# Tile 0 of a sparse graph-attention kernel: from the dense path to four list tiles made of column strips

## The chip, the cores and the metric

The kernel runs on one core of a Trainium2 chip. Its time is what one execution takes on the device, in microseconds (us). Three executions of the kernel before took 2577.2, 2580.97 and 2586.93 us; the median is 2580.97 us. One more execution was profiled, and its rows are the ones read here. Engines are called PE (TensorE), DVE (VectorE), ACT (ScalarE), POOL (GpSimd) and SP (the queue that only issues DMAs).

## The reference

`x` is 8192x256, `adj` 8192x8192 and mostly zero. With `h = relu(layernorm(x))` the layer is graph attention with 8 heads of 32:

```python
h = (x @ W.T).reshape(n, H, D)
s_src = einsum('nhd,hd->nh', h, a_src); s_dst = einsum('nhd,hd->nh', h, a_dst)
attn = s_src[:, None, :] + s_dst[None, :, :] + adj[:, :, None] * We[:, 0] + be
attn = where(adj[:, :, None] > 0, attn, -inf)
attn = softmax(leaky_relu(attn, 0.2), axis=1)
return x + einsum('ijh,jhd->ihd', attn, h).reshape(n, 256) + x @ Wr.T + br      # x in "x @" is relu(layernorm(x))
```

The probability of an edge between rows i and j falls with both numbers (as 1/sqrt of each). So row 0 has 738 neighbours, and the largest counts of tiles 0 to 11 (128 rows each) are 738, 75, 61, 58, 50, 43, 41, 39, 35, 36, 35 and 29. Within a row the neighbours are dense on the left and sparse on the right.

## The kernel before

**Prologue.** 32 steps of 256 rows each. DVE normalizes (`normalize`, lines 561 to 580), PE transposes and multiplies (`turn`, `maps`, lines 1047 to 1073), ACT copies out of PSUM, DVE adds the biases (`add_biases`, line 582), POOL stores the rows of `table` (features and destination scores), of `dst_rows` (the same scores transposed, for the dense path), of `resid` and of `out`. DVE and PE of neighbouring steps overlap.

**List tiles.** Tiles 1 to 63 are sparse enough for lists. For each, SP loads its 4 MB of `adj` in 8 pieces into one of two buffers. DVE *finds* (line 614): it cuts the 8192 columns into 7 to 35 segments, takes the 8 largest of each (line 632) with their columns (line 624) and packs them into keys (lines 636 to 651). It *sorts* (line 653): K//8+1 rounds over the keys give up to K neighbours a row. If a segment or the list might have held more, the tile's flag is set.

**Dealing.** From tile 4 on, tiles stand in groups (line 46). DVE counts the rows' neighbours (`count`, 690) and ranks them (`place`, 713, with matmuls at 1103), POOL scatters the lists by rank to HBM (`deal`, 514) and loads them back (`load_dealt`, 524). So the rows with the most neighbours share a tile, and the later tiles of the group have shorter lists: the K values in `GROUPS`. Tiles 1, 2 and 3 (`DIRECT`) are not dealt; they take 75, 61 and 58 slots.

**Units.** A list tile, dealt or direct, is a unit u. POOL gathers K table rows for each of the 128 rows of the unit, one indirect DMA a slot (`gather`, 488; line 500), into a ring of 86 slots. A slot is free when the matmuls that summed its last content are done; at most four gathers are in flight. ACT prepares the scores, DVE does the softmax in steps (`softmax_step`, 732) and multiplies most slots by their weights (`weight`, 762, line 769), ACT the rest (961), PE sums the slots (1085), DVE evacuates (772), POOL adds the result into `out` (`store`, 505, line 509), three units late.

**The order.** All orders are written out. DVE's loop (lines 784 to 812) does, for unit u, finds until `found[u]` tiles are found (table `FOUND`, line 57, then u+13), the last of them interleaved with unit u's softmax. `plan` (line 112) fixes after which unit's gather a group is dealt and loaded. POOL's loop is at 535.

**Dense path.** Tile 0 keeps its flag at 1 from the start (line 435). At the end the flags are read (820, 320), and each flagged tile is computed against all 8192 columns, head by head (`dense_tile`, 408, 828, 974, 1142). For these inputs that is tile 0 alone.

Of the kernel before, what the change touches and what calls it, by code (L numbers as in the profile page):

```python
# [22 lines left out]
P = 128  # L23
N = 8192
# [21 lines left out]
GROUPS = ((4, (50, 32, 28, 24)),  # L46
# [12 lines left out]
GMAX = max(len(ks) for _, ks in GROUPS)  # L59
KLIST = max(ks[0] for _, ks in GROUPS)  # L60
KMAX = 8 * (max(DIRECT) // 8 + 1)
VMAX = 8 * max(n for n, _ in SEGS.values())
WIDE = max(len(ks) * (HEAD + 2 * ks[0]) for _, ks in GROUPS)
RANKS = max(len(ks) * (ks[0] + 1) for _, ks in GROUPS)
# [6 lines left out]
class Source:  # L71


    def __init__(self, t, K, group, place):
        self.t, self.K, self.group, self.place = t, K, group, place
        self.segs, self.power = SEGS[max(a for a in SEGS if a <= t)]
        self.rounds = K // 8 + 1


class Unit:  # L80


    def __init__(self, u, K, source, group, place):
        self.u, self.K, self.source, self.group, self.place = u, K, source, group, place
        self.act_slots = K // 2 if K < 18 else 10 if K < 20 or K > 38 else 14 if K < 32 else 16
        self.parts = 2 if K < 30 else 3 if K < 40 else 8
# [15 lines left out]
class Group:  # L102


    def __init__(self, g, t0, ks):
        self.g, self.t0, self.ks, self.n, self.K = g, t0, ks, len(ks), ks[0]
        self.W, self.D = HEAD + 2 * ks[0], ks[0] + 1
        self.first = t0 - FIRST
        self.listed = t0 + self.n - FIRST


def plan():
    sources = [Source(FIRST + i, K, None, None) for i, K in enumerate(DIRECT)]
    units = [Unit(i, K, sources[i], None, None) for i, K in enumerate(DIRECT)]
    groups = []
    for g, (t0, ks) in enumerate(GROUPS):
        group = Group(g, t0, ks)
        groups.append(group)
        for i, K in enumerate(ks):
            sources.append(Source(t0 + i, group.K, group, i))  # L120
            units.append(Unit(len(units), K, None, group, i))

    found = [FOUND[u] if u < len(FOUND) else min(len(sources), u + LEAD) for u in range(len(units))]
    for group in groups:
        group.ranked_at = min(u for u in range(len(units)) if found[u] >= group.listed)
        group.placed_at = min(group.ranked_at + 1, group.first - 2)
        group.at_once = group.placed_at == group.ranked_at
# [3 lines left out]
    at, owner, part_sums, acts, issued = 0, [None] * GSLOTS, 0, 0, 0  # L131
    for un in units:
# [14 lines left out]
        if un.u >= LATE:  # L147
            units[un.u - LATE].store_seq = issued
            issued += 1
        for group in groups:  # L150
# [9 lines left out]
    return sources, units, groups, found  # L160
# [10 lines left out]
def gat_kernel(nc, x, adj, W, We, be, a_src, a_dst, Wr, br, out):  # L171
    table = nc.dram_tensor("table", (N + PAD, ROW), F32, kind="Internal").ap()
    resid = nc.dram_tensor("resid", (N, HD), F32, kind="Internal").ap()
    dst_rows = nc.dram_tensor("dst_rows", (H, N), F32, kind="Internal").ap()

    with ExitStack() as ctx:
        sources, units, groups, found = plan()
# [13 lines left out]
        ps_dst = banks[:, 2:6, 384:512].rearrange("p (u b) n -> p u b n", u=2)  # L191
# [14 lines left out]
        br_all = sb("br_all", [P, HD])  # L206
        be_all = sb("be_all", [P, H])
        we_all = sb("we_all", [P, H])
        seg_base = {(n, w): sb(f"seg_base{n}_{int(10 * w)}", [P, n * 8]) for n, w in sorted({(so.segs, so.power) for so in sources})}
# [17 lines left out]
        own = [sb(f"own{i}", [P, HEAD + 2 * K]) for i, K in enumerate(DIRECT)]  # L227
# [9 lines left out]
        limits = spare(len(GROUPS) * (KLIST + 1)).rearrange("p (g d) -> p g d", d=KLIST + 1)  # L237
        valid = spare(GMAX * KLIST)
# [23 lines left out]
        def part(width):  # L262
# [11 lines left out]
        dst_sb = part(2 * 2 * P).rearrange("p (u b n) -> p u b n", u=2, b=2)  # L274
# [22 lines left out]

        S = {n: sem(n) for n in (
            "ones_set", "held", "ident_set", "blk_zero", "blk_in", "w_in", "small_in", "wt_done", "wt_copied",
            "x_in0", "x_in1", "x_in2", "x_in3", "x_free", "bn_done", "mv_done", "sd_done", "eps_set", "rstd_done", "hn_done", "hnT_ps", "hnT_done",  # L300
            "proj_done", "hd_copied", "dst_copied", "s_done", "res_done", "br_added",
# [915 lines left out]
```

## Time and profile before

| | |
|---|---|
| median of 3 executions | 2580.97 us (2577.2 to 2586.93) |
| span of the profiled execution | 2582.7 us (the only figure there is for it; it stands 1.7 us above the median) |
| busy | DVE 2124.4 us (82%), POOL 1488.1 (58%), ACT 1246.3 (48%), PE 1240.2 (48%) |
| largest groups | gathers x1137 (line 500), segment maxima x624 (632) and their columns x624 (624) |
| DMA | 512.8 MB in 226533 packets, 199 GB/s mean |

The profile gives each engine's busy time and, for each instruction, the idle time before it with what ended it. POOL's busy time leaves out about 0.3 us between two gathers, which the rows call "issue": an engine 77% busy with gathers can be full. Stages are best read apart, since the engines' shares differ from one to the next.

### The profile page before, as it was taken

The numbers are of one execution on the slowest core, as the hardware profiler recorded it, in microseconds if no ns is written. First come the engines' busy times: TensorE is split into PE (matmuls) and PEld (weight loads), VectorE is DVE, ScalarE is ACT, GpSimd is POOL, SyncE is SP. The second block draws the span as 40 slices with busy tenths as digits, with TensorE's granted clock in tenths as the row PEclk, the third lists the DMA queues.
The fourth block names the chain that finished last, engine by engine and source line by source line (L and its number), as shares of the span: only waits on it lengthen the run. The fifth ranks groups of instructions, "written<-read, shape, count | busy, mean of one in ns | idle before, by whom it ended". The sixth has DMA issues, their size and how long they took to land.

```text
span 2582.7 us, 27816 instructions
## 1 busy us (share of the span) xinstructions
PE 1240.2 (48%) x5305; PEld 938.2 (36%) x5306; DVE 2124.4 (82%) x4852; ACT 1246.3 (48%) x4898; POOL 1488.1 (58%) x1666
## 2 busy tenths in 40 slices
PE   6991013504325267426634543443443364528885
PEld 4661013403314145314522432332332252416664
DVE  3558969999898998979998999999999921279991
ACT  1320030203335598639656555645634666826662
POOL 4772756656774677777777777656646657700000
PEclk9996557657656576656666665666666666759997
DMA  3667767686776877777787878778878424486660
GB/s 110 193 206 242 224 139 213 175 234 187 194 238 187 260 221 224 211 224 221 239 259 229 256 239 269 242 230 253 251 213 258 137 51 101 90 232 164 166 159 3
DMA packets 226533, 512.83 MB, mean 199 GB/s; under 512 B 98280, under 2 KB 116400, under 8 KB 224208
## 3 DMA queue, kind: packets, MB, share of 16 engines
q1 hardware_dynamic: 151280, 319.60, 39.2%
q0 software_dynamic: 74960, 191.61, 29.1%
q14 instruction: 116, 0.95, 0.1%
q8 instruction: 33, 0.54, 0.1%
q10 hardware_dynamic: 144, 0.13, 0.0%
HBM read 475.19 MB, written 36.03 MB: 198 GB/s over the span
## 4 chain that ended last, share of the span: by engine, by line
DMA 24%; issue 23%; DVE 12%; POOL 10%; PE 5%; ACT 4%; POOLq 0%; DVEq 0%; ACTq 0%; PEldq 0%; SPq 0%
DMA arena<-table,arena 18%; POOL arena L500 8%; DVE work L632 4%; ACT arena L961 3%; DMA out_dram<-w_all,arena 3%; DVE work L624 2%; PE banks L1115 1%; DMA lists<-arena,rank 1%; PE banks L1168 1%; DVE arena L769 1%; PE banks L1158 1%; DMA adj_sb<-in_adj_dram 1%; POOL lists L519 1%; DMA arena<-lists 1%; PE banks L1093 1%
## 5 line engine op out<-in xcount | busy, mean ns | idle before, releaser
L500 POOL DMA_INDIRECT arena<-table,arena x943 | 974.3, 1033 | 397.8 <-issue 237.3
L1093 PE MATMUL banks<-arena,ident 128*128 128x256 f32 x1268 | 420.2, 505 | 1030.7 <-DVE arena L769 1030.7
L961 ACT ACTIVATE arena<-arena,prob 128x32 f32<-128x32 f32 x4024 | 859.5, 306 | 2.0
L1093 PEld LDWEIGHTS banks<-arena,ident 128*128 128x128 f32 x1268 | 326.0, 263 | 1121.4 <-issue 884.4
L624 DVE FIND_INDEX8 work<-work,adj_sb 128x8 uint32<-128x184 f32 (+51 forms) x624 | 629.9, 1012 | 0.0
L632 DVE MAX8 work<-adj_sb 128x8 f32<-128x184 f32 (+51 forms) x624 | 620.4, 1002 | 0.7 <-DMA adj_sb<-in_adj_dram 0.4
L956 ACT ACTIVATE prob<-pre 128x104 f32<-128x104 f32 (+26 forms) x63 | 20.2, 321 | 866.4 <-DVE pre L753 866.4
L1099 PE MATMUL banks<-arena,ident 128*128 128x256 f32 x1006 | 317.4, 447 | 109.7 <-ACT arena L961 109.2
L500 POOL DMA_INDIRECT arena<-table,own x194 | 204.1, 1052 | 142.0 <-issue 47.4
L1099 PEld LDWEIGHTS banks<-arena,ident 128*128 128x128 f32 x1006 | 200.8, 216 | 215.0 <-ACT arena L961 192.5
L946 ACT ACTIVATE pre<-arena,we_all 128x13 f32<-128x13 f32 (+23 forms) x480 | 146.5, 400 | 78.6 <-DMA arena<-lists 78.6
L769 DVE TENSOR_TENSOR arena<-arena,prob 128x768 f32<-128x768 f32 (+7 forms) x158 | 183.1, 1208 | 0.0
L742 DVE TENSOR_TENSOR pre<-pre,arena 128x80 f32<-128x80 f32 (+20 forms) x76 | 19.8, 274 | 182.3 <-DMA arena<-table,arena 112.0
L509 POOL DMA_INDIRECT out_dram<-w_all,arena x60 | 98.5, 1642 | 44.2 <-DVE w_all L779 16.9
L519 POOL DMA_INDIRECT lists<-arena,rank x60 | 59.7, 996 | 110.2 <-DVE rank L726 86.6
L1115 PE MATMUL banks<-work,ones 128*128 128x24 f32 (+6 forms) x404 | 92.6, 384 | 0.0
L1115 PEld LDWEIGHTS banks<-work,ones 128*128 128x128 f32 x404 | 89.2, 323 | 0.0
L1168 PE MATMUL banks<-ident,adj_sb 128*128 128x128 f32 x256 | 44.7, 305 | 62.7 <-ACT adj_sb L989 62.7
L1072 PE MATMUL banks<-w_all,arena 128*128 128x256 f32 x256 | 73.0, 408 | 0.0
L1158 PE MATMUL banks<-pre,work 128*32 128x128 f32 x512 | 72.7, 289 | 0.0
L1066 PE MATMUL banks<-w_all,arena 128*128 128x272 f32 x256 | 70.1, 397 | 0.0
L850 DVE TENSOR_TENSOR arena<-arena 128x4096 f32<-128x4096 f32 x16 | 70.0, 4417 | 0.0
(140 smaller groups left out, 1795.8 us busy)
## 6 DMA issues: line engine op xcount, KB each, us to landing
adj_sb<-in_adj_dram SPq DMA_DIRECT2D x504, 512.0 KB, 4.5
arena<-dst_rows SPq DMA_DIRECT2D x16, 2048.0 KB, 8.7
arena<-table,arena POOLq DMA_INDIRECT x943, 4.1
table<-arena POOLq DMA_DIRECT2D x32, 264.0 KB, 2.9
arena<-in_x_dram SPq DMA_DIRECT2D x32, 256.0 KB, 3.0
resid<-arena POOLq DMA_DIRECT2D x32, 256.0 KB, 2.6
out_dram<-arena POOLq DMA_DIRECT2D x32, 256.0 KB, 2.8
work<-table SPq DMA_DIRECT2D x8, 1024.0 KB, 11.8
```

The costliest lines, as they stand in the source:

```text
L500: pool.indirect_dma_start(gath[:, un.slot(k), :], None, table[:, :], bass.IndirectOffsetOnAxis(ap=rec[:, k, 0:1], axis=0), bounds_check=N ...
L509: pool.indirect_dma_start(out[:, :], bass.IndirectOffsetOnAxis(ap=record(un)[:, 0:1].bitcast(U32), axis=0), out_sb[:, un.u % OUTS, :], Non ...
L519: pool.indirect_dma_start(lists[group.g][:, :], bass.IndirectOffsetOnAxis(ap=rank[:, group.g % 2, i:i + 1], axis=0), stage[:, group.g % 2, ...
L624: v.max_index(idx8[:, 8 * s:8 * s + 8], val8[:, 8 * s:8 * s + 8], a[:, bounds[s]:bounds[s + 1]]).then_inc(S["scanned"], 1)
L632: v.max(val8[:, 8 * s:8 * s + 8], a[:, bounds[s]:bounds[s + 1]]).then_inc(S["maxed"], 1)
L769: last = v.tensor_tensor(gv, gv, pb.unsqueeze(3).to_broadcast([P, n, H, D]), ALU.mult)
L946: last = s.activation(pv[:, h, :], pairs(rec, K)[:, :, 1], ACT.Identity, scale=we_all[:, h:h + 1], bias=rec[:, 1 + h:2 + h])
L961: last = s.activation(g, g, ACT.Copy, scale=prob[:, b, k * H + h:k * H + h + 1])
L1093: last = m.matmul(ps_sum[:, u % 2, :], ident[:, :], gath[:, un.slot(k), 0:HD], start=(k == 0), stop=False)
L1099: last = m.matmul(ps_sum[:, u % 2, :], ident[:, :], gath[:, un.slot(k), 0:HD], start=False, stop=(k == K - 1))
L1115: m.matmul(rv[:, i, :], ones[:, :], same[:, j * D:(j + 1) * D], start=False, stop=(i == n - 1 and j == i - 1))
L1158: last = m.matmul(ps_acc[:, b, :], hv[:, 4 * q + r, :], pt_sb[q % 4][:, r * P:(r + 1) * P], start=(q == 0 and r == 0), stop=(q == 15 and r ...
```

## The change

Tile 0 no longer goes through the dense path. Its 128 rows are cut into pieces of a row: rows 0 to 7 into 16 column strips, rows 8 to 23 into 8, rows 24 to 47 into 4, rows 48 to 127 into 2 (strip edges at N·w²/n², so that each holds about as many neighbours). The 512 pieces (cut into 37, 29, 46 and 39 segments over 992, 1920, 6144 and 6144 columns for the finds) are four list tiles ("windows") of 128 pieces each. Their sources stand first, as group 0 with K = 60, 37, 29, 22; tiles 1 to 3 become a dealt group with K = 75, 48, 39. The finds and sorts of the windows stand between the prologue's steps on DVE: steps 2 to 29 each get a seventh of one window. The window units store an unnormalized-by-tile result and the maxima and sums per head to HBM; after the last find, SP loads them by row, DVE and ACT combine the parts, and POOL adds the 128 rows to `out`. `dst_rows` is no longer written in the prologue (its matmuls, line 1069, its copy, 918, and its DMA, 467, are gone); the dense path, if a tile is flagged, would fetch it from `table`. The prologue's loops on SP and DVE are unrolled. Both `adj` buffers are set to zero on POOL at the start, and POOL fills 151 more 8-column segment bases there; before its first work DVE adds each piece's first column to them, in 17 one-column operations and 4 wide ones that wait for POOL's `ids`. Counted on the reference's matrix, no piece has more than 60 neighbours, no segment of a window that is checked has more than 7, and the rows above each K are at most as many as the tiles before it hold (124 of 128, 242 of 256, 371 of 384 for the windows; 122 of 128 and 246 of 256 for tiles 1 to 3).

```diff
+WINDOWS = (((0, 8, 16),), ((8, 24, 8),), ((24, 48, 4), (48, 64, 2)), ((64, 128, 2),))
+WINDOW_AT = ((0, 6144), (1, 6144), (0, 0), (1, 0))
+WINDOW_K = (60, 37, 29, 22)
...
+WINDOW_EXACT = (4, 1, 1, 0)
...
-GROUPS = ((4, (50, 32, 28, 24)),
+GROUPS = ((1, (75, 48, 39)),
+          (4, (50, 32, 28, 24)),
-DIRECT = (75, 61, 58)
-FOUND = (4, 7, 10, 12, 15, 16, 18, 20, 21, 22)
+FOUND = (7, 9, 10, 11, 14, 16, 18, 20, 21, 22)
...
-        group.placed_at = min(group.ranked_at + 1, group.first - 2)
+        group.placed_at = group.ranked_at + 1
```

On SP:

```diff
+            for u in range(4):
+                load_x(u)
+            sp.wait_ge(S["window_zero"], 2)
+            for k in range(NV):
+                so = sources[k]
+                for p, r0, r1, c0, c1 in so.windows():
+                    sp.dma_start(adj_sb[p:p + r1 - r0, so.buf, so.col:so.col + c1 - c0], adj[r0:r1, c0:c1]
+                                 ).then_inc(S[f"window_in{k}"], 16)
+            for u in range(4, 8):
+                load_x(u)
+            sp.wait_ge(S["s_done"], 1)
+            sp.dma_start(own_scores[:, :], s_all[:, 0, :]).then_inc(S["own_out"], 16)
+            sp.wait_ge(S["own_out"], 16)
+            for k in range(NV):
+                for p, r0, r1, c0, c1 in sources[k].windows():
+                    sp.dma_start(window_scores[p:p + r1 - r0, k, :], own_scores[r0:r1, :]).then_inc(S["own_in"], 16)
+            for u in range(8, UNITS):
+                load_x(u)
```

On POOL:

```diff
-            pool.memset(flags[:, :], 1.0).then_inc(S["flag_init"], 1)
+            for so in sources[:NV]:
+                for n in range(so.segs):
+                    last = pool.memset(window_base[so.c][:, 8 * n:8 * n + 8], float((so.bounds[n] + PAD) << JBITS))
+            for b in range(2):
+                pool.memset(adj_sb[:, b, :], 0.0).then_inc(S["window_zero"], 1)
-                    pool.wait_ge(S["dst_copied"], u + 1)
-                    pool.dma_start(dst_rows[:, bass.ts(u, 2 * P)].rearrange("h (b p) -> h b p", b=2),
-                                   dst_sb[0:H, q, :, :]).then_inc(S[f"dst_out{q}"], 16)
+            deal(groups[0])
+            load_dealt(groups[0])
             for un in units:
                 gather(un)
                 if un.u >= LATE:
                     store(units[un.u - LATE])
+                if un.u == comb_store_at:
+                    pool.wait_ge(S["comb_done"], 1)
+                    pool.dma_start(out[0:P, :], comb_out, accum_op=ALU.add).then_inc(S["comb_out"], 16)
```

On DVE:

```diff
+            dve.wait_ge(S["ids_set"], 1)
...
+            def windows_beside(u):
+                c, m = (u - 2) // 7, (u - 2) % 7
+                if u < 2 or c >= NV:
+                    return
+                segs, steps = sources[c].segs, 2 * sources[c].rounds
+                if m < 4:
+                    scan(c, segs * m // 4, segs * (m + 1) // 4)
+                if m == 4:
+                    keys(c)
+                if m >= 4:
+                    for step in range(steps * (m - 4) // 3, steps * (m - 3) // 3):
+                        sort_step(c, step)
+                if m == 6:
+                    decode(c)
+
+            for u in range(UNITS):
+                normalize(u, u % 4)
+                windows_beside(u)
+                if u >= 2:
+                    add_biases(u - 2, (u - 2) % 4)
+            add_biases(UNITS - 2, 2)
+            count(groups[0])
+            add_biases(UNITS - 1, 3)
+            place(groups[0])
...
+                if un.u == comb_clear_at:
+                    combine_clear()
+                if un.u == comb_shift_at:
+                    combine_shift()
+                if un.u == comb_out_at:
+                    combine_out()
```

On PE:

```diff
-                    for c in range(2):
-                        rows = hnT[:, q, b, c * P:(c + 1) * P]
-                        m.matmul(ps_dst[0:H, q, b, :], w_all[:, c, HD:ROW], rows, start=(c == 0), stop=(c == 1))
```

## Rows read from the trace of the kernel before

**Rows 1.** Busy time of each engine, PE clock and DMA by stage.

```profile
core 0: us, PE busy (x) PEld busy (x) DVE busy (x) ACT busy (x) POOL busy (x), PEclk, DMA share, GB/s
...
20.30:206.90 186.60, 178.79 (x896) 123.25 (x896) 90.39 (x288) 54.24 (x129) 125.16 (x156) 1.00 0.60 193
206.90:822.00 615.10, 173.58 (x712) 148.24 (x712) 566.20 (x1621) 143.32 (x627) 368.32 (x352) 0.62 0.71 199
822.00:1154.00 332.00, 151.98 (x482) 109.33 (x482) 294.80 (x707) 215.49 (x975) 237.80 (x226) 0.63 0.76 232
1154.00:2010.00 856.00, 388.63 (x1262) 292.46 (x1262) 833.96 (x1844) 500.58 (x2239) 576.52 (x542) 0.64 0.80 242
2010.00:2266.00 256.00, 128.49 (x394) 94.74 (x393) 98.54 (x267) 170.15 (x754) 170.13 (x156) 0.66 0.37 88
2266.00:2582.60 316.60, 215.19 (x1544) 166.80 (x1544) 238.87 (x121) 162.51 (x176) 0.00 (x0) 0.84 0.58 147
```

**Rows 2.** Timeline around 2262 us: the last store, then the dense tile's first load.

```profile
2262.05 1.57 POOL L509 DMA_INDIRECT out_dram<-w_all,arena  x1 [3.55 <-DVE w_all L779]
...
2266.15 0.34 SPq L411 DMA_DIRECT2D adj_sb<-in_adj_dram  x1
```

**Rows 3.** Timeline of DVE, one step of the prologue to the next.

```profile
47.84 0.75 DVE L566 BATCH_NORM_STATS2 arena<-arena 128x6 f32<-128x256 f32 x2 [0.38 <-DVE arena L591]
...
52.04 0.17 DVE L585 TENSOR_TENSOR s_all<-arena,be_all 128x16 f32 x1 [1.75 <-ACT arena L917]
...
53.24 0.43 DVE L566 BATCH_NORM_STATS2 arena<-arena 128x6 f32<-128x256 f32 x1 [0.36 <-DVE arena L591]
```

**Rows 4.** Timeline of PE in one such step.

```profile
61.79 0.60 PE L1052 MATMUL banks<-ident,arena 128*128 128x128 f32 x4
...
63.24 0.60 PE L1069 MATMUL banks<-arena,w_all 128*8 128x128 f32 x4
63.77 1.13 PE L1072 MATMUL banks<-w_all,arena 128*128 128x256 f32 x4
```

**Rows 5.** Timeline of DVE: find and sort of tile 1, end of tile 2's find.

```profile
207.00 0.24 DVE L632 MAX8 work<-adj_sb 128x8 f32<-128x8 f32 x2 [0.45 <-DMA adj_sb<-in_adj_dram]
...
230.71 0.19 DVE L636 TENSOR_REDUCE flag<-work 128x1 f32<-128x35 f32 x1
...
232.63 0.45 DVE L662 MAX8 work<-work 128x8 f32<-128x280 f32 x1
...
250.40 0.26 DVE L632 MAX8 work<-adj_sb 128x8 f32<-128x12 f32 x2
...
272.39 0.17 DVE L636 TENSOR_REDUCE flag<-work 128x1 f32<-128x26 f32 x1
```

**Rows 6.** Timeline of POOL at the start.

```profile
0.92 0.20 POOL L432 MEMSET ones<- 128x128 f32 x1 [0.29 <-POOLq L1204]
...
1.24 5.37 POOL L439 MEMSET seg_base<- 128x8 f32 x155
```

**Rows 7.** Gathers (line 500) by stretch: POOL busy time, their count, clock, DMA.

```profile
251.00:358.00 107.00, 75.32 (x76) 0.50 0.76 211
358.00:557.70 199.70, 128.77 (x119) 0.65 0.69 179
572.00:780.00 208.00, 140.36 (x134) 0.66 0.74 211
```

**Rows 8.** Timeline of POOL: the deal and the load before tile 8.

```profile
801.36 1.02 POOL L519 DMA_INDIRECT lists<-arena,rank  x1 [20.34 <-DVE rank L726]
...
816.04 0.95 POOL L532 DMA_DIRECT2D arena<-lists  x1 [3.93 <-DMA lists<-arena,rank]
...
821.84 1.06 POOL L500 DMA_INDIRECT arena<-table,arena  x1 [4.84 <-DMA arena<-lists]
```

**Rows 9.** The page's groups: stores of a unit, and DVE's weighting.

```profile
L769 DVE TENSOR_TENSOR arena<-arena,prob 128x768 f32<-128x768 f32 (+7 forms) x158 | 183.1, 1208 | 0.0
...
L509 POOL DMA_INDIRECT out_dram<-w_all,arena x60 | 98.5, 1642 | 44.2 <-DVE w_all L779 16.9
```

More of the change, by code:

```diff
@@ L147, in plan @@
         if un.u >= LATE:
-            units[un.u - LATE].store_seq = issued
-            issued += 1
-        for group in groups:
+            done = units[un.u - LATE]
+            done.store_seq = issued
+            issued += 2 if done.partial else 1
+        for group in groups[1:]:
             if group.dealt_after == un.u:
@@ L159, in plan @@
         issued += 1
-    return sources, units, groups, found
+    return sources, units, groups, found, issued
 def segments(n, power):
@@ L352, in listed, with own_head, loads_before @@
         def listed(eng, un):
-            if un.group is None:
-                eng.wait_ge(S["decoded"], un.u + 1)
-            else:
-                landed(eng, un.group.load_seq + 1)
+            landed(eng, un.group.load_seq + 1)
+        def own_head(group):
+            if group.t0 is None:
+                return ids[:, 0:NV], window_scores[:, :, :], window_flags[:, :]
+            rows = slice(group.t0, group.t0 + group.n)
+            return ids[:, rows], s_all[:, rows, :], flags[:, rows]
         segs_before = [sum(so.segs for so in sources[:c]) for c in range(len(sources))]
         def scans_of(so, n):
-            return sum(lo < (n + 1) * PIECE for lo in segments(so.segs, so.power)[:-1])
+            return sum(lo < (n + 1) * PIECE for lo in so.bounds[:-1])
+        def loads_before(so):
+            return sum(o.t is not None and o.buf == so.buf for o in sources[:so.c])
+        last_find = min(u for u in range(len(units)) if found[u] == len(sources))
+        comb_clear_at, comb_shift_at, comb_out_at, comb_store_at = (last_find + i for i in (0, 2, 3, 5))
         load_adj = lambda t: adj[bass.ts(t, P), :]
@@ L674, in decode @@
                 t, K, rec = so.t, so.K, staged(so)
-                if so.group is not None and so.place == 0 and so.group.g >= 2:
+                if so.place == 0 and so.group.g >= 2:
                     before = groups[so.group.g - 2]
@@ L686, in decode @@
                 dve.wait_ge(S["flag_a"], c + 1)
-                v.tensor_tensor(flags[:, t:t + 1], flag8[:, :], slot_lo[:, K:K + 1].bitcast(F32), ALU.max
+                flag = own_head(so.group)[2][:, so.place:so.place + 1]
+                v.tensor_tensor(flag, flag8[:, :], slot_lo[:, K:K + 1].bitcast(F32), ALU.max
                                 ).then_inc(S["flag_b"], 1)
@@ L784, in _ @@
             for un in units:
-                at_once = [group for group in groups if group.at_once and group.ranked_at == un.u]
-                while done_finds < found[un.u] - (not at_once):
+                while done_finds < found[un.u] - 1:
                     find(done_finds)
@@ L791, in _ @@
                     done_finds += 1
-                for group in at_once:
-                    count(group)
                 c = done_finds if done_finds < found[un.u] else None
```

337 lines of the change are left out of this document (220 added, 117 removed), and 9 rows, old and new, of the table WINDOW_SEGS.

## The prediction

> **What bounds the kernel now.** I read the stages first [rows 1], then the end [rows 2], the gathers by stretch [rows 7], and single timelines for prices. The rows show four regimes. In the prologue (20.3 to 206.9 us) PE is busy 178.8 of 186.6 us and DVE only 90.4: PE sets the step of 186.6/32 = 5.83 us. From 206.9 to 822 DVE is busy 92%, with finds running ahead of the first units, whose gathers POOL starts at 251. From 822 to 1154, where the lists are dealt but still long, DVE falls to 89% while POOL has 226 operations in 332 us; each takes about 1.02 us and leaves 0.3 us between two, so 1.3 us at best and 1.47 us here: POOL is full and DVE waits for its gathers. From 1154 to 2010 DVE is busy 97%. After the last find POOL is again the slower one, to the last store at 2262 [rows 2]. Then the dense tile has the chip to itself from 2266.2 to the end of the span, 316.5 us, in which POOL does nothing [rows 1, 2].
>
> **The dense tile: -314 us.** Nothing lies beside it, so all 316.5 us go if no tile is flagged. The counts on the reference's matrix say that none is: 60 neighbours at most in a piece, 7 at most in a checked segment, and every K has room for its ranks. The engines still read the flags beside the landing of the last store; I put 2 us on that (0 to 5).
>
> **The start: +16 us.** POOL's segment bases cost 5.37 us for 155, 0.035 each started one behind the other; 151 more are 5.3 us. Zeroing both buffers is two writes 8192 wide: 128 columns took 0.20 us and 8 columns about 0.10, so 0.8 ns a column and 6.6 us each [rows 6]. The ids that DVE now waits for come behind both, 18.5 us later than the bases' old end at 6.6 plus 0.5 us of small work: at 25.6. DVE's 21 small operations, most in a chain of dependent ones, I put at 0.3 us each: 6 us. The weights' copies, at 14.5 us before, thus wait until about 31. Bounds: 5 (if the zeroing overlaps or is faster) to 20.
>
> **The prologue's steps: +79 us.** Removed is line 1069 on PE: 0.53 us twice a step [rows 4], so PE needs 5.83 - 1.06 = 4.8 us. Also gone are one ACT copy and one POOL DMA a step; neither engine bound, so they are worth nothing. Added on DVE is the work of four windows. Finds: tile 1's 35 segments took 23.7 us and tile 2's 26 took 22.0, both over 8192 columns [rows 5]; so 0.19 us a segment and 2.08 ns a column. The windows have 151 segments and 15200 columns: 28.7 + 31.6 = 60 us. Keys: 1.92 us at 280 wide [rows 5]; four of 232 to 368, 8 us. Sorts: tile 1's ten rounds took 17.8 us [rows 5], 1.78 each; 4 x 8 rounds, a little wider on average, at 1.9: 61 us. Decoding 2 us. Sum 131 us, or 4.7 in each of 28 steps. DVE's own part of a step is 53.24 - 47.84 = 5.40 us less 1.75 of waiting for ACT [rows 3], 3.65 us. So DVE becomes the bound: 28 x 8.35 = 234, the other four steps at 5.4 = 22, and count, rank and place of group 0, about 25 small operations and one round over PE, 8: 264 instead of 186.6, +77. SP issues 32 window loads and, later, 32 score loads between the loads of x; x(8) stands behind the second lot. At 0.5 us an issue that is 16 us, while x(8) is due three steps (25 us) after they can start: nearly hidden, 2 us. Prologue and start end DVE's part at 207 + 16 + 79 = 302 us, +95. Bounds +65 (131 us partly filling waits that I count twice, a cheap start) to +125.
>
> Here a rule speaks against the change. The clock in the prologue was 1.00, PE's 2.4 GHz level, with PE busy 96%; in the list stages, with PE busy 28 to 50%, its mean was 0.62 to 0.66; in the dense stage, at 68%, 0.84 [rows 1]. After the change PE is busy 4.8 of 8.35 us, and much of each step is one idle stretch. The Trainium skill, "TensorE: Matmul & The Clock Gate", section "Part 1: The HAM clock gate", says that a stretch without matmuls puts the array back to half rate until it has been busy again. By that rule the steps would partly run at the 1.2 GHz level, and with PE as the bound the sum would be some 25 us longer, inside my range. The rows alone give the price: 4.8 us at the lower level is 9.6 us, against 8.35 for DVE; a mix of the two levels, as the dense stage shows it, stays under 8.35, so I add nothing.
>
> **POOL's queue up to tile 8: +134 us on top.** Before, tile 8's first gather began at 821.84 [rows 8], 615 us after the prologue. In the new order, counted from DVE's end of the prologue: POOL's last stores of the prologue 6; four deals, landing and load, 15 (from 801.36 to 821.84 eight deals and one load took 20.5 [rows 8]): 21. 148 window gathers: the 76 from 251 us on took 1.41 us each with nothing in their way, the next 119 took 1.68 with ring waits and slow landings [rows 7]; the windows lie between, nearer the first because their predecessors are short: 1.45, 215 us. Two stores of the first window, 1.64 + 0.3 each [rows 9], three deals and a load: 14. 162 gathers of tiles 1 to 3 at 1.55 (the mean of both stretches was 1.58), 251. Stores of three windows, 12, and the deal and load of the next group, 11. So tile 4 starts at +524. Tiles 4 to 7 took 208 us [rows 7]; deal and load for tile 8 then take 17, without the 20.3 us that POOL waited for DVE's ranks [rows 8], since those are now made a unit earlier and DVE is ahead. 749 against 615: +134. Bounds: 85 (all at 1.41) to 165 (all at 1.68).
>
> DVE's own addition in this stage is small: the windows put 94 slots on it and tiles 1 to 3 take 32 off; at 1.208/3 = 0.40 us a slot [rows 9] that is 25 us, softmax steps some 5 us. So DVE idles for what POOL is later. From tile 8 on, orders, lead and K values are as before; POOL was the bound there until 1154 and DVE, in lockstep with it, after. I see no place where 134 us would be won back.
>
> **The combining: +2 us.** It has two operations 4096 wide, 6.4 us each by the 1.208 us of a 768 wide one [rows 9], and small ones, and lies after the last find, where DVE is busy 98.5 of 256 us. POOL waits for it two units later. If that cover were gone it would cost 15 us. ACT's added share (54 slots) has room: 143 of 615 us busy.
>
> **Sum,** against the profiled execution: 2582.7 - 314 + 16 + 79 + 134 + 2 = 2500 us. I round to 2495, which also takes off the 1.7 us by which the median of the three runs is lower.
>
> **Rivals.**
> - *Finds hide the gathers (15%).* If POOL's queue is no bound up to tile 8, because DVE's finds take the time anyway (92% busy there), only DVE's 30 us come on top instead of 134: 2390 us. For it: DVE's share up to 822. Against: 116 more gathers have no room in a stretch where POOL's 352 operations, at 1.3 us each, already fill 458 of the 571 us from 251 to 822 [rows 1].
> - *Slow gathers (13%).* The early gathers all run at the 1.68 us of the second stretch [rows 7], since SP's loads of adj take the same DMA engines (0.71 busy): 310 x 0.15 = 46 more, 2541 us.
> - *Lockstep in the prologue (5%), the slower side.* DVE's chunk, 8.35 us, and PE's part at the lower clock, 9.6, stand one behind the other in each step instead of side by side, in that DVE waits in `normalize` or `add_biases` for what PE could only start after the chunk. Then a step is 18 us, 28 x 9.6 = 270 us more: 2765. It makes the kernel slower as soon as a step passes about 11.5 us. Against it: `add_biases(u-2)` and `normalize(u)` ask for results of two steps back.
> - *The dense tile runs after all (2%).* A flag stays set; then 316 us return with a slow fetch of the transposed scores: over 2811 us.
> - The forecast: 60%. The other 5% are mishaps between these.
>
> **How the numbers follow.** The forecast's own bounds are 2495 - 30 - 49 = 2416 and 2495 + 30 + 31 = 2556, and with the slow gathers 2541 lies inside. The finds-hide case at 2390 is left out with the slower ones: 2415 to 2555 holds about 75 to 80%. About 0.5%, 13 us, is what a measurement of this kernel can tell from no change. Faster by more than that (below 2568): 60 + 15 + 13 + part of the rest = 91%, of which I keep 0.89; within 0.5%, 0.03; slower 0.08.
>
> **What the profile would show.** Right: no instruction of the dense lines; DVE near 90% busy in the prologue, its steps about 8.3 us, ending near 300 us; PE's clock there at or under 1.00; first gather near 323 us; tile 4's first gather near 825, tile 8's near 1050; DVE waiting for gathers up to tile 16; the last find near 2240 and the last store near 2495. Wrong: a prologue that ends after 330 or a step over 10 us; gathers at 1.6 us or more; DVE with no idle time before the softmax of tiles 1 to 7, in which case the time would be nearer 2390.

## The result, and the profile after

The change makes the kernel faster: 2503.4 us (median of 4 executions, 2501.01 to 2509.92) against 2583.66 for the kernel before beside it. The ratio is 0.9694, 95% interval [0.9674, 0.9714]. The forecast was 2495, its range 2415 to 2555. Some executions of a kernel are over 1.5% longer than its fastest; the ratios leave these out, the medians don't. The profiled execution has a span of 2500.6 us, 82.1 less than before.

Stages of the kernel after: the prologue; up to tile 4's first gather; up to tile 8's; up to the end of the stretch in which DVE waits for gathers; up to about the last finds; the tail. The columns are those of [rows 1].

```profile
core 0: us, PE busy (x) PEld busy (x) DVE busy (x) ACT busy (x) POOL busy (x), PEclk, DMA share, GB/s
35.00:295.00 260.00, 164.70 (x666) 130.81 (x666) 212.50 (x971) 43.77 (x97) 109.82 (x128) 0.87 0.51 157
295.00:824.00 529.00, 143.77 (x586) 120.43 (x586) 487.22 (x1454) 149.19 (x658) 349.55 (x332) 0.62 0.69 203
824.00:1047.00 223.00, 93.34 (x376) 75.16 (x376) 158.37 (x361) 97.40 (x439) 159.50 (x148) 0.66 0.63 181
1047.00:1380.00 333.00, 150.86 (x483) 108.99 (x483) 253.42 (x608) 218.97 (x992) 243.72 (x231) 0.63 0.69 205
1380.00:2240.00 860.00, 392.45 (x1279) 292.23 (x1280) 838.71 (x1856) 508.57 (x2275) 578.86 (x544) 0.64 0.80 243
2240.00:2491.00 251.00, 118.38 (x378) 88.29 (x376) 104.72 (x237) 158.63 (x703) 167.35 (x150) 0.66 0.36 81
```

The dense stage of [rows 1] has no counterpart. The prologue took 186.6 us and takes 260, with DVE busy 82% instead of 48%. From 824 to 1380 DVE, which was about 90% busy in those tiles before, is at 74%.

The next rows come from the timelines of DVE and POOL in the kernel after. They are DVE's first step and its first find behind the prologue, then POOL's first window gather, its first gathers of tiles 4 and 8 (line 596), and its last store.

```profile
35.09 0.74 DVE L702 BATCH_NORM_STATS2 arena<-arena 128x6 f32<-128x256 f32 x2
...
294.90 0.23 DVE L753 MAX8 work<-adj_sb 128x8 f32<-128x8 f32 x2
```

```profile
317.21 1.05 POOL L596 DMA_INDIRECT arena<-table,arena  x1 [7.42 <-DMA arena<-lists]
...
824.18 1.06 POOL L596 DMA_INDIRECT arena<-table,arena  x1 [4.14 <-issue]
...
1046.59 1.06 POOL L596 DMA_INDIRECT arena<-table,arena  x1 [4.43 <-issue]
...
2485.15 1.56 POOL L615 DMA_INDIRECT out_dram<-w_all,arena  x1 [3.15 <-DVE w_all L914]
```

They give the ledger. The left column is what the sum of the prediction had.

| term | forecast | measured, from the rows |
|---|---|---|
| DVE starts later | +16 | 35.09 - 20.3 = +14.8 |
| the prologue's steps and group 0's ranks | +79 | (294.90 - 35.09) - (207.00 - 20.3) = +73.1 |
| POOL's queue from there to tile 8 | +134 | (1046.59 - 294.90) - (821.84 - 207.00) = +136.9 |
| from tile 8 to the last store | +2 | (2485.15 - 1046.59) - (2262.05 - 821.84) = -1.7 |
| after the last store | -314 | (2500.6 - 2485.15) - (2582.7 - 2262.05) = -305.2 |
| sum | -83 (2500, given as 2495) | -82.1 |

Whether each term's reason holds is another matter, and that took the experiments.

### The profile page after: what moved, and what is told of

Its sections match the earlier page's. It is cut to its first block, busy times and chain, and to the rows that moved or that the text cites. A ratio compares the mean times of both kernels' runs of the same rounds, so it can differ in the third digit from the quotient of the medians.

```text
span 2500.6 us, 24906 instructions
## 1 busy us (share of the span) xinstructions
PE 1067.0 (43%) x3781; PEld 819.3 (33%) x3782; DVE 2061.7 (82%) x5509; ACT 1176.6 (47%) x5159; POOL 1638.2 (66%) x1929
## 3 DMA queue, kind: packets, MB, share of 16 engines
q14 instruction: 132, 1.08, 0.1%
## 4 chain that ended last, share of the span: by engine, by line
DMA 20%; issue 17%; POOL 10%; DVE 6%; ACT 2%; PE 2%; POOLq 0%; DVEq 0%; ACTq 0%
DMA arena<-table,arena 17%; POOL arena L596 9%; ACT arena L1160 2%; DVE work L753 2%; DMA out_dram<-w_all,arena 2%; DVE work L742 1%; PE banks L1314 1%; POOL lists L625 1%; PE banks L1292 1%; DMA lists<-arena,rank 1%; DVE arena L904 1%; POOL out_dram L615 0%; POOLq L596 0%; PE banks L1312 0%; PE banks L1298 0%
## 5 line engine op out<-in xcount | busy, mean ns | idle before, releaser
L596 POOL DMA_INDIRECT arena<-table,arena x1253 | 1308.7, 1044 | 533.5 <-issue 329.3
L1292 PE MATMUL banks<-arena,ident 128*128 128x256 f32 x1392 | 454.0, 500 | 1170.7 <-DVE arena L904 1170.7
L1160 ACT ACTIVATE arena<-arena,prob 128x32 f32<-128x32 f32 x4456 | 951.5, 307 | 2.2
L1292 PEld LDWEIGHTS banks<-arena,ident 128*128 128x128 f32 x1392 | 354.4, 260 | 1268.1 <-issue 1018.8
L742 DVE FIND_INDEX8 work<-work,adj_sb 128x8 uint32<-128x502 f32 (+56 forms) x775 | 669.7, 866 | 0.0
L753 DVE MAX8 work<-adj_sb 128x8 f32<-128x502 f32 (+56 forms) x775 | 658.6, 857 | 0.0
L1298 PE MATMUL banks<-arena,ident 128*128 128x256 f32 x1114 | 347.2, 444 | 121.2 <-ACT arena L1160 120.6
L1298 PEld LDWEIGHTS banks<-arena,ident 128*128 128x128 f32 x1114 | 219.1, 213 | 236.0 <-ACT arena L1160 212.7
L1145 ACT ACTIVATE pre<-arena,we_all 128x13 f32<-128x13 f32 (+27 forms) x536 | 165.1, 406 | 104.5 <-DMA arena<-lists 104.5
L904 DVE TENSOR_TENSOR arena<-arena,prob 128x768 f32<-128x768 f32 (+8 forms) x166 | 200.7, 1258 | 0.0
L1314 PE MATMUL banks<-work,ones 128*128 128x24 f32 (+8 forms) x422 | 90.0, 365 | 0.0
L795 DVE MAX8 work<-work 128x8 f32<-128x56 f32 (+11 forms) x290 | 81.4, 281 | 5.3
L796 DVE MAX8 work<-work 128x8 f32<-128x56 f32 (+11 forms) x290 | 77.0, 266 | 0.0
## 6 DMA issues: line engine op xcount, KB each, us to landing
adj_sb<-in_adj_dram SPq DMA_DIRECT2D x1, 1536.0 KB, 23.1
```

The costliest lines, as they stand in the source:

```text
L596: pool.indirect_dma_start(gath[:, un.slot(k), :], None, table[:, :], bass.IndirectOffsetOnAxis(ap=rec[:, k, 0:1], axis=0), bounds_check=N ...
L742: v.max_index(idx8[:, 8 * s:8 * s + 8], val8[:, 8 * s:8 * s + 8], a[:, bounds[s]:bounds[s + 1]]).then_inc(S["scanned"], 1)
L753: v.max(val8[:, 8 * s:8 * s + 8], a[:, bounds[s]:bounds[s + 1]]).then_inc(S["maxed"], 1)
L904: last = v.tensor_tensor(gv, gv, pb.unsqueeze(3).to_broadcast([P, n, H, D]), ALU.mult)
L1145: last = s.activation(pv[:, h, :], pairs(rec, K)[:, :, 1], ACT.Identity, scale=we_all[:, h:h + 1], bias=rec[:, 1 + h:2 + h])
L1160: last = s.activation(g, g, ACT.Copy, scale=prob[:, b, k * H + h:k * H + h + 1])
```

## The experiments

Their line numbers are their own; some differ from those of the kernel after by one or more.

**1. The dense path alone, taken out of the kernel before.**

```diff
-            pool.memset(flags[:, :], 1.0).then_inc(S["flag_init"], 1)
+            pool.memset(flags[:, :], 0.0).then_inc(S["flag_init"], 1)
```

> The kernel before, with tile 0's flag at 0 from the start: the attention part of tile 0 is left out and nothing else changes. Mine: the dense stage costs 316.5 us less what the engines then still do after the last store. In the kernel after, 13.9 us lie between the last store's end (2486.7) and the span's end (2500.6); with the same here the span is 2263.6 + 13.9 = 2277.5 us (2272 to 2283). Rival, the prediction's own term: only 2 us remain after the landing at 2266, so 2268 us.

Measured: 2290.61 us against 2589.29 for the kernel before beside it, ratio 0.8833 [0.8808, 0.8859], 298.7 us less. The profile has a span of 2289.9 us and this last store:

```profile
2274.56 1.57 POOL L509 DMA_INDIRECT out_dram<-w_all,arena  x1 [3.56 <-DVE w_all L779]
```

From its end to the span's end are 13.8 us, as in the kernel after (13.9), so the expectation's reason holds, though the span lies outside its 2272 to 2283: the list stage itself ran 12.5 us longer in this execution than in [rows 2], for a reason that I don't know. Removing the dense path is worth some 300 us, and the rest of the change gives 220 of them back: 0.9694 - 0.8833 = 0.0861 of 2589.

**2. Without the loop that reads the flags,** and without the dense path's code behind it.

```diff
         def flagged_tiles(eng, body):
+            return
```

> The kernel after, without the loop that reads the flags and without the dense path behind it (nothing is flagged, so the output is the same). Mine: the loop's eight reads per engine are what follows the last store's landing; without them the span ends some 5 us after the last store, 2491 us, 9 us less. Rival: the end is a fixed cost of every execution (the landing and the program's end), and 2500 us stay.

Measured: 2502.53 us, ratio 0.9656 [0.9633, 0.9678], against 0.9694 [0.9674, 0.9714] for the kernel after; the intervals overlap. The trace tells more. The last store starts at 2484.59 and the span is 2494.9 us:

```profile
2484.59 1.56 POOL L616 DMA_INDIRECT out_dram<-w_all,arena  x1 [3.14 <-DVE w_all L915]
```

So 8.8 us remain behind the store instead of 13.9. Of the end, 5 us are the loop with its branch over the dense path (I expected 9); the rest is the landing and the end of the program.

**3. Half of the windows' gathers.**

```diff
-WINDOW_K = (60, 37, 29, 22)
+WINDOW_K = (30, 19, 15, 11)
-        self.rounds = self.K // 8 + 1
+        self.rounds = 8 if t is None else self.K // 8 + 1
-                v.tensor_scalar(flag_row[:, :], ps_flag_row[0:1, 0:TILES], 0.0, None, ALU.is_gt)
+                v.tensor_scalar(flag_row[:, :], ps_flag_row[0:1, 0:TILES], 3e38, None, ALU.is_gt)
```

> The kernel after with the windows' lists cut to K = 30, 19, 15 and 11 (75 gathers instead of 148), eight sort rounds as before, and the flags ignored: tile 0 leaves out about half of its neighbours. Prologue unchanged. Mine (POOL's gathers bind up to tile 16, DVE idles there for some 150 us): 73 gathers at 1.45 us are 106 us less, most of which arrives: span 2385 to 2415 us. Rival (DVE's finds bind and hide the gathers): only DVE's weighting of about 55 slots at 0.31 us and a few us of softmax go: 2480 to 2487 us.

Measured: 2461.05 us, ratio 0.9494 [0.947, 0.9519], 0.0200 of 2589 = 52 us less than the kernel after by the ratios, 35 by the spans (2465.2). It lies between the two: neither was right. POOL's timeline shows where the gain went. This is the wait before tiles 1 to 3 are dealt, first in this kernel (with tile 1's first gather behind it), then in the kernel after:

```profile
482.52 1.03 POOL L625 DMA_INDIRECT lists<-arena,rank  x1 [76.04 <-DVE rank L859]
...
510.44 1.06 POOL L596 DMA_INDIRECT arena<-table,arena  x1 [5.05 <-DMA arena<-lists]
```

```profile
509.69 1.03 POOL L625 DMA_INDIRECT lists<-arena,rank  x1 [9.13 <-DVE rank L859]
```

The deal needs the ranks of tiles 1 to 3, and `place` for them stands on DVE behind the five finds (tiles 1 to 5) of units 0 and 1. In the kernel after, POOL is through with three windows' gathers at 500.6 us and DVE with its ranks at 508.9: the two paths are level. Halve the gathers and POOL waits 76 us. So at that deal DVE comes last, by 9 us, and nearly all of the windows' first 126 gathers are hidden behind finds. Not quite all: DVE's own path up to the deal holds one wait for POOL, before the first window's softmax, which the half windows don't have:

```profile
409.40 0.66 DVE L877 TENSOR_TENSOR pre<-pre,arena 128x480 f32<-128x480 f32 x1 [10.22 <-DMA arena<-table,arena]
```

The half's deal came 27 us earlier (482.5 instead of 509.7): 10 us are this wait, the other 17 are DVE's weighting (20.6 us by then against 7.4) and softmax. Some 9 us more go behind the deal, where the fourth window is shorter.

**4. Half of the windows' gathers, with the ranks asked for earlier.**

```diff
-FOUND = (7, 9, 10, 11, 14, 16, 18, 20, 21, 22)
+FOUND = (7, 7, 9, 11, 14, 16, 18, 20, 21, 22)
```

> As the half windows, with the second entry of FOUND at 7 instead of 9, so that no find stands in unit 1 and the ranks of tiles 1 to 3 come right after unit 0's and unit 1's softmax (tile 0 leaves out half of its neighbours again). In the half windows POOL waited 76 us for these ranks. Mine now: up to tile 1's softmax DVE's finds bind (it idled only some 15 us from 295 to 633 us there), and POOL's queue from there on; so the wait moves, and 10 to 25 us are gained against the half windows: 2438 to 2452. Rival (POOL's queue binds all the way, as the prediction had it): the 76 us shrink to about 20 and most of that arrives: 2405 to 2420.

Measured: 2466.62 us, ratio 0.9543 [0.9515, 0.9571], no faster than experiment 3. The deal came 49 us earlier:

```profile
433.04 1.03 POOL L625 DMA_INDIRECT lists<-arena,rank  x1 [27.02 <-DVE rank L859]
```

and tile 1's gathers ended 55 us earlier (570 us against 625), but its softmax stood where it had stood (632.81 us in experiment 3), since all the finds of the first ten tiles lie before it on DVE:

```profile
634.22 0.77 DVE L881 SCALAR_TENSOR_TENSOR pre<-pre 128x600 f32<-128x600 f32 x1
```

Behind it POOL has to wait, since the ring's slots come free only when tile 1's are summed. This is a gather of tile 2:

```profile
650.97 9.31 POOL L596 DMA_INDIRECT arena<-table,arena  x1 [60.15 <-PE banks L1292]
```

Both expectations fell, mine of 10 to 25 us too: with half the gathers, finds bind up to tile 1's softmax, and none of POOL's 49 us arrives behind it.

**5. The same order in the full kernel.**

```diff
-FOUND = (7, 9, 10, 11, 14, 16, 18, 20, 21, 22)
+FOUND = (7, 7, 9, 11, 14, 16, 18, 20, 21, 22)
```

> The kernel after with that entry of FOUND alone. POOL waits 9.1 us for the ranks of tiles 1 to 3, with DVE's path and POOL's path nearly level there. Mine: 5 to 12 us less, 2491 to 2498. Rival (finds bind throughout): no change, 2503.

Measured: 2513.96 us, ratio 0.9725 [0.9699, 0.9752], slower than the kernel after by 8 us by the ratios (the intervals overlap). A miss: POOL's 9.1 us are gone, but DVE, with no find in unit 1, waits for the second window's gathers:

```profile
DVE pre L877 <- DMA arena<-table,arena: 21.2, 1, 21.2
```

Here both engines are bounds: whichever is relieved waits for the other.

**6. The windows behind the prologue instead of between its steps.**

```diff
                 normalize(u, u % 4)
-                windows_beside(u)
                 if u >= 2:
                     add_biases(u - 2, (u - 2) % 4)
             add_biases(UNITS - 2, 2)
-            count(groups[0])
             add_biases(UNITS - 1, 3)
+            for u in range(2, 2 + 7 * NV):
+                windows_beside(u)
+            count(groups[0])
```

> The kernel after with the windows' finds, sorts and decodes all placed behind the prologue's last step instead of between its steps. Mine: PE sets the step again, at 4.8 to 5.0 us without line 1069's matmuls, so the steps end near 195 us, the windows add 131, group 0's ranks 6: DVE ends the prologue at 332 instead of 295 and the span is 2537 us (2525 to 2550). Rival (the clock falls and DVE waits for PE when interleaved, so nothing is hidden): the same 2500 us or less.

Measured: 2546.75 us, ratio 0.9833 [0.9808, 0.9857], 36 us more than the kernel after by the ratios. As expected. Busy times of the steps and of the windows by themselves:

```profile
35.00:200.00 165.00, 134.68 (x618) 108.54 (x619) 86.74 (x286) 45.02 (x95) 101.58 (x118) 0.92 0.70 206
200.00:340.00 140.00, 8.89 (x40) 7.71 (x38) 128.18 (x676) 1.25 (x2) 9.13 (x11) 0.53 0.25 78
```

The windows' own work on DVE ran from 206.7 to 333.7 us, 127 us where the sum had 131. Undisturbed steps took 4.2 us, with PE busy 97% of the time (from 120 to 190 us): without line 1069 PE needs 1.6 us less than the 5.83 of before, not 1.06. The interleaving thus saves about 36 of 127 us. Part of that isn't overlap of work with work: DVE waited 23.2 us for x here and 11.7 in the kernel after.

**7. x ahead of the windows in SP's queue.**

```diff
+            load_window(0)
+            for u in range(4, 7):
+                load_x(u)
+            load_window(1)
+            load_x(7)
...
             for u in range(8, UNITS):
                 load_x(u)
+                if u == 9:
+                    load_window(2)
+                if u == 11:
+                    load_window(3)
```

> The kernel after with SP's window loads spread: window 0 before x(4), window 1 before x(7), windows 2 and 3 behind x(9) and x(11). In the kernel after DVE waits 9.9 us for x(4) and 1.8 for x(8). Mine: x(4), asked for at 49 us, lay behind the 32 window loads on the DMA engines; spread, 9 to 12 us go, and all later stages shift by as much: 2492 us. Rival: the later steps have the slack (DVE idles 38 us in the prologue in all) and take it up, 2500 to 2503.

Why it was tried: in the kernel after, DVE stood here in its fifth step,

```profile
64.24 0.75 DVE L702 BATCH_NORM_STATS2 arena<-arena 128x6 f32<-128x256 f32 x2 [9.88 <-DMA arena<-in_x_dram]
```

for a load that SP had asked for at 49.23 us. Measured: 2507.48 us, ratio 0.97 [0.9677, 0.9722], the same as the kernel after. The wait moved. These are DVE's waits in the prologue, in the kernel after and here:

```profile
DVE arena L702 <- DMA arena<-in_x_dram: 11.7, 2, 9.9
...
DVE arena L725 <- DMA out_dram<-arena: 0.5, 1, 0.5
```

```profile
DVE arena L732 <- DMA out_dram<-arena: 6.1, 3, 4.7
DVE arena L709 <- DMA arena<-in_x_dram: 4.6, 4, 2.5
```

Together 12.2 us and 10.7. POOL's first window gather began at 317.38 instead of 317.21. The rival was right that nothing is gained, and not in its reason: no slack took up the wait, as much came back from other DMAs. That the windows' transfers now collide with these is likely and not shown.

**8. A longer lead of the finds.**

```diff
-FOUND = (7, 9, 10, 11, 14, 16, 18, 20, 21, 22)
-LEAD = 13
+FOUND = (7, 9, 10, 11, 14, 16, 18, 20, 22, 24, 26, 28)
+LEAD = 17
```

> The kernel after with finds up to 17 units ahead instead of 13 (FOUND from unit 8 on: 22, 24, 26, 28, then u+17). Mine: DVE idles some 150 us between 554 and 1380 us waiting for gathers, and stands 97% busy from 1380 to 2240; four finds (24 us each) move from the one to the other, the last find comes some 90 us earlier, and POOL's queue then takes up part: 2420 to 2460 us. Rival: the finds in the early stretch delay the weights that free ring slots, so POOL is later by what DVE gains: 2490 to 2503.

Measured: 2466.84 us, ratio 0.954 [0.9514, 0.9565]: 40 us less than the kernel after by the ratios, 43 by the spans, and 119 less than the kernel before. It is the fastest of the versions that leave nothing out. From 825 to 1051 us, where tiles 4 to 7 are gathered:

```profile
825.00:1051.00 226.00, 93.12 (x374) 76.07 (x374) 199.22 (x445) 96.38 (x436) 158.55 (x148) 0.65 0.73 207
```

DVE does 41 us more work here than the kernel after (199.22 against 158.37), and tile 8's first gather comes at 1050.98 instead of 1046.59:

```profile
1050.98 1.06 POOL L596 DMA_INDIRECT arena<-table,arena  x1 [6.88 <-DMA arena<-lists]
...
2441.65 1.56 POOL L615 DMA_INDIRECT out_dram<-w_all,arena  x1 [3.16 <-DVE w_all L914]
```

That is direct evidence that POOL's queue binds in these tiles: DVE had nearly all of that time to give away. Nearly, since the delay grows to 17 us by tile 10's store (1277.1 against 1260.5) and stays at 10 to 16 us up to the ranks of a later group. The gain comes behind that, at three deals. In the kernel after POOL waits for the ranks there; with the longer lead it waits for none of the three (0.30 us before each deal):

```profile
1912.04 1.02 POOL L625 DMA_INDIRECT lists<-arena,rank  x1 [18.74 <-DVE rank L859]
...
2113.17 1.02 POOL L625 DMA_INDIRECT lists<-arena,rank  x1 [25.23 <-DVE rank L859]
...
2308.43 1.46 POOL L625 DMA_INDIRECT lists<-arena,rank  x1 [20.39 <-issue]
```

(The third row gives no releaser; in experiment 3 the same deal waits 17.9 us for DVE's ranks.) These are 64 us, and what is left of them at the last store is 43.5. The kernel before waits at the same three deals:

```profile
1693.64 1.03 POOL L519 DMA_INDIRECT lists<-arena,rank  x1 [20.28 <-DVE rank L726]
...
1894.60 1.04 POOL L519 DMA_INDIRECT lists<-arena,rank  x1 [24.18 <-DVE rank L726]
...
2089.78 1.02 POOL L519 DMA_INDIRECT lists<-arena,rank  x1 [19.95 <-DVE rank L726]
```

So the waits that the longer lead removes are not new with the change; experiment 10 asks what it is worth without it.

**9 to 12.** The last four kernels ran on another chip. The kernel before beside them took 2707.27 us there (2680.3 to 2761.63), so their times aren't comparable with those above. What slows that chip isn't known. The traces show that ACT, PE and DVE stand still at many places behind the prologue, for a reason that the profile doesn't see. This is ACT's exponential in the kernel after, then in experiment 9 ("issue" is idle time without a known end):

```profile
L1155 ACT ACTIVATE prob<-pre 128x120 f32<-128x120 f32 (+21 forms) x67 | 21.8, 325 | 955.7 <-DVE pre L888 955.7
```

```profile
L1155 ACT ACTIVATE prob<-pre 128x120 f32<-128x120 f32 (+21 forms) x67 | 21.6, 322 | 891.5 <-DVE pre L888 610.2 <-issue 281.4
```

The four kernels are told by their ratios and by the stages before these stops.

*9, finds 18 units ahead:*

```diff
-FOUND = (7, 9, 10, 11, 14, 16, 18, 20, 21, 22)
-LEAD = 13
+FOUND = (7, 9, 10, 11, 15, 17, 19, 22, 24, 26, 28, 29)
+LEAD = 18
```

> The kernel after with finds 18 units ahead, and one more find before tiles 1 and 3 already (FOUND 7, 9, 10, 11, 15, 17, 19, 22, 24, 26, 28, 29, then u+18). With 17 the last gather ended 43 us earlier than in the kernel after, and DVE still idled some 50 us before the softmax of tiles 1 to 3. Mine: one find (24 us) more moves into that idle time; 10 to 25 us less than the 2467 of the 17: 2442 to 2457. Rival (POOL's queue is the bound throughout by now): 2460 to 2467.

Measured: 2693.36 us, ratio 0.9887 [0.9794, 0.998]; inconclusive. DVE had no idle time before the maxima of its finds, so it didn't lack `adj`. Its longest wait with an unknown end is the one for ACT's exponentials:

```profile
DVE rsum L892 <- remote: 118.8, 7, 36.5
```

*10, the longer lead in the kernel before:*

```diff
-FOUND = (4, 7, 10, 12, 15, 16, 18, 20, 21, 22)
-LEAD = 13
+FOUND = (4, 7, 10, 12, 15, 16, 18, 21, 23, 25)
+LEAD = 17
```

> The kernel before with finds 17 units ahead (FOUND 21, 23, 25 for units 7 to 9, then u+17), to tell what the longer lead is worth without the change. Before, DVE idled 45 us for gathers from 906 to 1221 us, and POOL waited 20 to 24 us for ranks four times. Mine: the room is smaller than after the change; 10 to 25 us less: 2560 to 2577 on the scale of 2587. Rival (the lead is worth the same in both): 38 us less, 2549.

Measured: 2702.55 us, ratio 0.9977 [0.9938, 1.0016], no difference that can be told. In its trace POOL waits at none of the three deals any more, and waits for DVE's evacuations instead (144 us in 16 waits before stores, where the kernel before had 17). With the stops of this chip on top, it doesn't show a gain and doesn't exclude one on the other: how much of experiment 8's 40 us the kernel before could have had stays open.

*11, more work for PE in the prologue:*

```diff
                     for c in range(2):
                         rows = hnT[:, q, b, c * P:(c + 1) * P]
-                        last = m.matmul(ps_res[:, q, b, :], rows, w_all[:, c, 272:528], start=(c == 0), stop=(c == 1))
+                        m.matmul(ps_res[:, q, b, :], rows, w_all[:, c, 272:528], start=(c == 0), stop=(c == 1))
+                    for c in range(2):
+                        rows = hnT[:, q, b, c * P:(c + 1) * P]
+                        last = m.matmul(ps_res[:, q, b, :], rows, w_all[:, c, 272:528], start=(c == 0), stop=(c == 1))
```

> The kernel after with each residual matmul of the prologue done twice (the second overwrites the first): PE's work in a step goes from 4.8 to 6.7 us at the 2.4 GHz level. Mine: DVE sets the step (82% busy), the clock rises from 0.86 because PE idles less, and the prologue ends where it did: 2500 to 2506. Rival (PE at the lower level binds in part of the steps): 2 us more in each of those, 2515 to 2560.

Measured: 2705.21 us, ratio 0.9824 [0.9745, 0.9903], inconclusive as a time. The prologue lies before the stops and can be read:

```profile
35.00:295.00 260.00, 208.38 (x896) 172.13 (x896) 210.55 (x960) 44.25 (x97) 106.52 (x124) 0.91 0.50 151
```

PE is busy 208 us instead of 165, and most steps are what they were: of the 31 intervals from one step of DVE to the next, 25 are within 0.1 us of the kernel after's. The other six, all among the first twelve, differ by 0.2 to 1.2 us and add up to 3 us; the first window gather came at 322 instead of 317 us. So DVE sets the step, but for a few early ones that wait for PE's results.

*12, without the combining:*

```diff
-                if un.u == comb_clear_at:
-                    combine_clear()
-                if un.u == comb_shift_at:
-                    combine_shift()
-                if un.u == comb_out_at:
-                    combine_out()
...
-                if un.u == comb_store_at:
-                    pool.wait_ge(S["comb_done"], 1)
-                    pool.dma_start(out[0:P, :], comb_out, accum_op=ALU.add).then_inc(S["comb_out"], 16)
```

> The kernel after without the combining (its clearing, loads, seven DVE operations, the exponential and the added store; tile 0's attention part is left out, its stores to HBM stay). In the trace after, one gather took 4.96 us instead of 1.00 beside the 4.42 us of the 4096 wide multiply, and one store waited 10.0 us for DVE. Mine: 3 to 10 us less, since POOL's queue binds there. Rival (hidden, the prediction's 2 us): no difference that can be told from 2503.

Measured: 2690.23 us, inconclusive. The two undisturbed traces bound the price instead: from the first gather of the unit with K = 8 of the last group but one to the last store it is 2262.05 - 2100.55 = 161.5 us before and 2485.15 - 2319.22 = 165.9 after, so 4.4 us, where the sum had 2. The same stretch took 163.1 us in experiment 1, so some 1.5 us of the 4.4 can be chance.

## Why the prediction was right, point by point

**The dense tile** went, and so did its price; nothing was flagged. The term was 9 us too good. The sum put 2 us (0 to 5) behind the last landing; 13.9 us lie behind the last store, of which experiment 2 gives 5 to the loop that reads the flags and the branch behind it. Before, the dense path's start at 2266.15 [rows 2] hid this end.

**The start** was 14.8 against 16. The two zeroings took 13.8 us on POOL (13.2 forecast), and DVE waited for the ids to 26.17 us (25.6).

**The prologue's steps** were right in mechanism: DVE sets them (82% busy where I had put near 90; experiment 11), the windows cost 127 us (experiment 6; 131 forecast), and an average step took (294.9 - 35.1)/32 = 8.1 us. The 28 with a part of a window were uneven, 4.6 to 15 us, as the windows' sevenths are. PE's own step was mis-sized, 4.2 us instead of 4.8 (experiment 6), which costs nothing as long as DVE sets the step. Wrong was the part on SP's queue: I took x(8) for the load at risk and 2 us for the price; x(4) was late by 9.9 us, not behind the issues, which took 12.8 us in all, but behind the windows' transfers. And in experiment 7 another order of the loads didn't win it back.

**The clock.** In the prologue it was 0.87 on average, with PE busy 165 of 260 us; in one step

```profile
185.53 1.11 PE L1254 MATMUL banks<-ident,arena 128*128 128x128 f32 x4 [8.12 <-DVE arena L714]
186.44 2.02 PE L1268 MATMUL banks<-w_all,arena 128*128 128x272 f32 x4
...
189.65 1.08 PE L1268 MATMUL banks<-w_all,arena 128*128 128x272 f32 x4
```

the same four matmuls took 2.02 us after 8 us of waiting (granted clock 0.50, the 1.2 GHz level) and 1.08 three microseconds later (1.00, the 2.4 GHz level). By the rule that the prediction cites from the Trainium skill, "TensorE: Matmul & The Clock Gate", section "Part 1: The HAM clock gate", the idle stretch puts the array back and work brings it up; the trace agrees. The 25 us did not come, since at this mix PE stays under DVE's step, as the sum had it from the rows.

**POOL's queue up to tile 8** came out at +136.9 against +134, first gather at 317 (323), tile 4 at 824 (825), tile 8 at 1047 (1050). The number was right, and the reason for its first part only by half. The step that failed is "148 window gathers ... 1.45, 215 us" as the bound from the prologue's end on. Experiments 3 and 4 show that DVE's three plus two finds and two softmaxes need as long as POOL's gathers of three windows: 508.9 and 500.6 us at the deal. The sum did not compare the two paths there, and they happened to be level; that the number came out is in this part luck. Had the windows been half as long, the same sum would have promised 106 us and 35 to 52 would have come. From tile 1's gathers on the reason holds: DVE waits before all but one of the softmaxes of tiles 1 to 11 (4 to 27 us each; tile 3's is the one), and 41 us more of finds delay tile 8 by 4 us (experiment 8). The term's upper bound was summed wrongly: 310 gathers at 1.68 us are 521 us, 55 more than the 466 of the sum, so "all at 1.68" is +189 and not +165, and the slow-gathers rival by the same count 2550 instead of 2541.

**"I see no place where 134 us would be won back"**: none was. From tile 8 to the last store the kernel took 1.7 us less, with the combining's 4.4 in it (experiment 12; the sum had 2). But the sentence reads as if nothing could be done. A longer lead takes 40 us, by putting finds into DVE's new idle time and so removing three waits for ranks; the waits themselves are older than the change, and how much the lead needs the new idle time is open (experiment 10).

**The rivals.** Finds-hide (2390) fell as a whole and is right, but for 10 us, for the stretch up to the first deal. Slow gathers fell: the window gathers took 1.42 to 1.48 us each, tiles 1 to 3 took 1.42 to 1.53. Lockstep fell. Nothing was flagged.

## What to carry to other kernels

Where work is added to an engine's queue, compare the other engine's path at each point where the two meet (here: the first deal), not only the queue with itself; a sum along one queue can give the right end while another path binds. When a change makes one engine wait, look for what that engine could do earlier: here a constant in the order of the finds gave 40 us more. And a stage that is removed from the end uncovers what it hid, here 11 us of the program's own end: 15.4 us from the last store to the end, where the dense tile had begun 4.1 us behind it.

## What the runs showed of the hardware that I had not expected

Beside DVE's multiply of two SBUF operands, 4096 wide, one gather of POOL took 4.96 us instead of 1.00; beside the reduction that follows, of one operand and longer, the gathers ran as ever:

```profile
2336.42 4.42 DVE L946 TENSOR_TENSOR adj_sb<-adj_sb 128x4096 f32<-128x4096 f32 x1
2336.76 4.96 POOL L596 DMA_INDIRECT arena<-table,arena  x1 [0.30 <-PE banks L1292]
...
2340.88 7.01 DVE L949 TENSOR_REDUCE adj_sb<-adj_sb 128x256 f32<-128x4096 f32 x1
2342.02 1.00 POOL L596 DMA_INDIRECT arena<-table,arena  x1 [0.30 <-issue]
2343.32 0.99 POOL L596 DMA_INDIRECT arena<-table,arena  x1 [0.30 <-issue]
```

The gather began 0.34 us behind the multiply and ended 0.9 us after it (2341.72 against 2340.84), so it stood still for the rest of the DVE instruction. The longest gather took 4.95 to 5.13 us in seven more kernels with this multiply, and 2.50 in experiment 12, which leaves it out. The weighting (line 904), also a multiply of two SBUF operands, does the same on a small scale: the 113 gathers that ran mostly beside it took 1.41 us on average, up to 3.08, and the 398 beside the finds' MAX8 took 1.00. In experiment 4 six weightings stood one behind the other for 13.56 us, and the gather in them took 9.31 us. The Trainium skill, "GPSIMD Engine Reference", section "1. Specifications", says that GpSimd shares its SBUF interfaces with VectorE and that the two get in each other's way when a VectorE instruction has two SBUF inputs. These rows agree. The 4 us that the one gather lost are about the combining's 4.4.

The largest window load (64 rows of `adj` by 6144 columns, 1536 KB) landed 23.1 us after its issue, and x(4), asked for behind it, 15 us after its own (49.23 to 64.21), where the median for x is 2.7 us.
